# A window-attention and wavelet-convolution kernel: the keys' scaling moves from VectorE to GpSimd

## The reference, cut to what matters

```python
qkv = einsum('oc,bchw->bohw', w_qkv, gn(x))     # then cut into 16x16 windows and 8 heads of 12 channels
q = l2norm(q)                                   # over the 12 channels of a head
k = l2norm(k)                                   # k / |k|
ksum = k.sum(axis=-1) + 1e-6                    # over the 256 pixels of a window
tailor = 1.0 / (256 + einsum('bhnc,bhc->bhn', q, ksum))
kv = einsum('bhmn,bhcn->bhmc', k, v)
attn = (einsum('bhnm,bhmc->bhcn', q, kv) + v.sum(-1)) * tailor
y = batchnorm(einsum('oc,bchw->bohw', w_proj, attn)) * gamma + beta
x = x + y                                       # then layer 1
```

## Time and profile before

| | |
|---|---|
| runs | 11306.57, 11311.51, 11315.59 us (median 11311.51) |
| the profiled execution | 11311.75 us, of which the span is 11309.9 us |
| PE busy | 10853.3 us, 96% |
| DVE busy | 9314.2 us, 82% |
| ACT busy | 6979.7 us, 62% |
| POOL busy | 3419.9 us, 30% |
| attention block, first to last copy to `tok` | 131.7 to 5506.9 us |

### The profile page before, as it was taken

The page is one execution under the profiler, slowest core; times in us unless marked ns, Lnnn a source line. Parts: engine busy times, 40 slices in busy tenths (PEclk is TensorE's granted clock), DMA queues, the critical chain, the costliest instruction groups (busy, mean ns, idle before and its releaser), DMA issues.

```text
span 11309.9 us, 208798 instructions
## 1 busy us (share of the span) xinstructions
PE 10853.3 (96%) x68772; PEld 9284.1 (82%) x68772; DVE 9314.2 (82%) x16092; ACT 6979.7 (62%) x11660; POOL 3419.9 (30%) x2756
## 2 busy tenths in 40 slices
PE   4999999999999999999599999999999999999999
PEld 4888888888888888888588888888888888888888
DVE  6989999899998989988677777777777777777777
ACT  4777777777777777788445445454454545545454
POOL 3444444344444444444222122212222122221221
PEclk9999999999999999999799999999999999999999
DMA  5333233233333333222266666666666766667665
GB/s 184 126 101 125 96 123 123 92 129 101 114 114 116 113 101 130 93 80 81 73 140 151 148 148 147 145 153 147 149 145 145 154 146 150 144 146 153 145 150 118
DMA packets 1149039, 1453.41 MB, mean 129 GB/s; under 512 B 201567, under 2 KB 1111199, under 8 KB 1111455
## 3 DMA queue, kind: packets, MB, share of 16 engines
q1 hardware_dynamic: 1147231, 1442.74, 50.1%
q10 hardware_dynamic: 1376, 6.13, 0.1%
HBM read 1040.06 MB, written 408.56 MB: 128 GB/s over the span
## 4 chain that ended last, share of the span: by engine, by line
PE 49%; DVE 1%; SPq 0%; DMA 0%; issue 0%; POOL 0%; DVEq 0%; POOLq 0%
PE ps_w L1274 10%; PE ps_w L1275 10%; PE ps_w L1276 10%; PE ps_ll L1282 4%; PE ps L1274 4%; PE ps L1275 4%; PE ps L1276 4%; PE ps_w L1317 4%; DVE ob L1399 0%; DVE x L1337 0%; DMA yb<-y_scratch 0%; SPq L1101 0%; SPq L1110 0%; DMA prm<-params 0%; SPq L1120 0%
## 5 line engine op out<-in xcount | busy, mean ns | idle before, releaser
L1274 PE MATMUL ps_w<-zb,mat 128*128 128x512 f32 x4800 | 1925.7, 401 | 1.6 <-DVE ob L1399 1.6
L1276 PE MATMUL ps_w<-zb,mat 128*128 128x512 f32 x4800 | 1907.6, 397 | 0.0
L1275 PE MATMUL ps_w<-zb,mat 128*128 128x512 f32 x4800 | 1907.2, 397 | 0.0
L1227 ACT ACTIVATE z<-x,prm 64x384 f32<-64x384 f32 (+1 forms) x3072 | 1807.2, 659 | 55.5 <-DVE x L1337 47.8
L635 POOL CAST xn_hi<-xs 96x512 fp32r<-96x512 f32 x1024 | 842.7, 823 | 3106.9 <-PE ps_qkv L660 2255.4
L1173 POOL CAST mat<-raw 128x1280 fp32r<-128x1280 f32 (+1 forms) x288 | 344.8, 1215 | 4454.8 <-DMA raw<-vec 2674.2
L1399 DVE SCALAR_TENSOR_TENSOR ob<-ps_w,prm,x 64x512 f32<-64x512 f32 x1920 | 1440.6, 750 | 148.7 <-PE ps_w L1317 109.5
L1337 DVE SCALAR_TENSOR_TENSOR x<-yb,prm,xb 128x1024 f32<-128x1024 f32 (+1 forms) x576 | 1120.4, 1997 | 421.6 <-DMA prm<-params 374.9
L658 PE MATMUL ps_qkv<-wqkv_hi,xn_hi 96*128 96x288 f32 x4096 | 1388.4, 339 | 38.0 <-POOL xn_lo L637 19.8
L637 POOL TENSOR_TENSOR xn_lo<-xs,xn_hi 96x512 fp32r<-96x512 f32 x1024 | 1363.7, 1332 | 81.9
L1247 ACT ACTIVATE ll<-ps_ll 128x512 f32<-128x512 f32 x192 | 115.1, 599 | 1880.5 <-PE ps_ll L1282 1880.5
(11 more groups left out here) (183 smaller groups left out, 24815.2 us busy)
## 6 DMA issues: line engine op xcount, KB each, us to landing
xst<-in_x SPq DMA_DIRECT2D x96, 2048.0 KB, 13.8
xs<-in_x SPq DMA_DIRECT2D x128, 1536.0 KB, 8.9
y_scratch<-ys SPq DMA_DIRECT2D x128, 1536.0 KB, 9.5
out<-ob SPq DMA_DIRECT2D x768, 208.0 KB
xb<-in_x SPq DMA_DIRECT2D x576, 256.0 KB
yb<-y_scratch SPq DMA_DIRECT2D x576, 256.0 KB
raw<-vec SPq DMA_DIRECT2D x192, 320.0 KB, 5.4
raw<-vec SPq DMA_DIRECT2D x384, 160.0 KB, 4.2
```

What stands on the lines that cost most here:

```text
L1227: last = nc.scalar.activation(z[q * WROWS:(q + 1) * WROWS, ts, b, :], x1[slot(k, g)][rows, pairs, b, q::2], ACT.Identity, scale=prm[k][row ...
L1274: mm(out_, w[HI], xx[HI], start=start, stop=False)
L1275: mm(out_, w[HI], xx[LO], start=False, stop=False)
L1276: return mm(out_, w[LO], xx[HI], start=False, stop=stop)
```

## The change

Three things. `unit_k` is cut in two: DVE keeps the reciprocal (`invert_k`), and the multiplication goes to POOL, under the old name. POOL's step becomes unit_k(u-1) and then halves(u+2), where it was halves(u+1); the wait that halves makes for a slot is as before. And ACT normalises the next strip's four chunks in the steps j = 0, 1, 2, 3, where it was 0, 2, 4, 6. `invert_k` has one wait more, for POOL's multiplication of the pair before, which reads `rk`.

```diff
@@ ACT, step
-                    if j % 2 == 0 and inside_(at, -PAIRS) and (at is None or at < LAST - PAIRS):
+                    if j < 4 and (at is None or at < LAST - PAIRS):
...
-                        normalise(n + 1, (k + 1) % XS, j // 2)
+                        normalise(n + 1, (k + 1) % XS, j)
@@ POOL
+                def unit_k(u, slot):
+                    pool.wait_ge(krec_ready, u + 1)
+                    pool.wait_ge(tok_copied, u + 1)
+                    k = tok[:, slot, :, PART:PART + C].rearrange("p g (h c) -> p g h c", c=HD)
+                    nc.gpsimd.tensor_tensor(k, k, rk[:].unsqueeze(3).to_broadcast([128, TG, NH, HD]), ALU.mult
+                                            ).then_inc(khat_ready, 1)
...
                 def step(b, m, k, j, at, extra, stats):
                     n = b * STRIPS_IMG + m * XS + k
-                    if at is None or at + 1 < LAST:
-                        nn, kk = (n, k) if j + 1 < PAIRS else (n + 1, (k + 1) % XS)
-                        halves(n * PAIRS + (j + 1), nn, kk, (j + 1) % PAIRS, at is not None and at + 1 < 2)
+                    if inside_(at, 1):
+                        unit_k(n * PAIRS + (j - 1), (j - 1) % 2)
+                    if at is None or at + 2 < LAST:
+                        nn, kk = (n, k) if j + 2 < PAIRS else (n + 1, (k + 1) % XS)
+                        halves(n * PAIRS + (j + 2), nn, kk, (j + 2) % PAIRS, False)
 
                 halves(0, 0, 0, 0, True)
+                halves(1, 0, 0, 1, True)
@@ DVE
-                def unit_k(u, slot):
+                def invert_k(u, slot, first):
                     dve.wait_ge(norm_ready, u + 1)
+                    if not first:
+                        dve.wait_ge(khat_ready, u)
                     v.reciprocal(rk[:], tok[:, slot, :, QR:PART]).then_inc(krec_ready, 1)
-                    dve.wait_ge(krec_ready, u + 1)
-                    dve.wait_ge(tok_copied, u + 1)
-                    k = tok[:, slot, :, PART:PART + C].rearrange("p g (h c) -> p g h c", c=HD)
-                    v.tensor_tensor(k, k, rk[:].unsqueeze(3).to_broadcast([128, TG, NH, HD]), ALU.mult
-                                    ).then_inc(khat_ready, 1)
...
-                        unit_k(u - 1, (j - 1) % 2)
+                        invert_k(u - 1, (j - 1) % 2, at == 1)
```

## The result

The changed kernel takes 11429.79 us (median of 5 runs, 11425.38 to 11447.96) against 11315.59 (5 runs, 11306.57 to 11317.82): a ratio of 1.0105, 95% interval 1.0092 to 1.0119. It is slower, by 114 us between the medians; 405 were forecast, and the time lies 0.2 us under the lower end of the range. The profiled execution has a span of 11429.0 us, 119 more than before.

A forecast was written before the change was run, and what follows sets the result against it. PE was taken to bound the kernel, with odd steps of loaded strips bound by reciprocal, multiplication, kv_sums. Terms 94 + 55 + 276 - 20 = +405 on 11311.5 gave about 11716 us, range 11430 to 11850.

The forecast's parts named there:

- The bound: Attention block: PE bounds it, and in odd steps of loaded strips the way reciprocal, multiplication, kv_sums, making a step 0.61 longer.
- The clash with even j: Even j, every strip: count_xy on DVE blocks POOL's multiplication, so PE waits; +0.54 each, 512 times, +276 us.
- The length of the multiplication: POOL's multiplication of 384 elements: 0.99 us, from a line through L637 and a 25-element operation of the same kind.
- POOL's wake: POOL's start behind the instruction that releases it: 0.19 us, read from normalise and the cast it released.
- odd j, loaded: Odd steps of loaded strips: keys ready at 3070.92 instead of 3070.64, +0.28 each, 336 times, +94 us.
- Odd j, plain: Odd steps of plain strips: slack gone, +0.24 and 0.07 for the wait, 176 times, +55 us.
- -20: Start of each strip: earlier normalise lets the first casts come at their usual time; 0.16 x 128 = 20 us given back.
- No clash: Rival for even j: multiplication and count_xy run side by side, the even term goes; 11441 us, chance 0.12.
- POOL first: Rival for even j: POOL wins the shared path, count_xy ends 1.08 later, odd keys are late; 11711 us, chance 0.15.
- Faster: Rival: POOL multiplies at the cast's rate, 0.46 us, odd keys in loaded strips 0.25 earlier; 11208 us, chance 0.11.
- Covered and free: POOL's casts behind the multiplication, invert_k's new wait and normalise in j 0 to 3: hidden, costing nothing.
- The bounds: POOL's multiplication: 0.46 us at the cast's rate to 1.38 at that of L1178.

The follow-up runs named there:

- keys_first: The kernel before with one edit: with odd j, DVE makes the keys ahead of the two bn_stats on y; 11192.0 us, ratio 0.9888.
- mult_back: The changed kernel with the multiplication of the keys alone put back on DVE; 11297.88 us, ratio 0.9984 to the kernel before.
- one_input: The changed kernel with count_xy's product of two SBUF operands replaced by a sum over one operand; 11306.29 us, ratio 0.9993.
- keys_first_early: The edits of mult_back and keys_first together, multiplication on DVE, normalise in j 0 to 3; 11098.16 us, ratio 0.981.
- keys_first_pool: The changed kernel, multiplication on POOL, with the keys ahead of the bn_stats with odd j; 11273.07 us, ratio 0.9964.

## Why the prediction was right or wrong

**The bound** was read rightly. PE waits for keys in the odd steps of loaded strips, and the way to them is reciprocal, multiplication, `kv_sums`: keys_first took what stands ahead of that way and the wait was gone. That freeing DVE behind the reciprocal gains nothing held too: 673 us of DVE's work bought nothing.

**The clash with even j** was right as a mechanism: `count_xy` first, 0.27 behind the reciprocal, POOL behind it, with 0.15 of its start hidden in the wait (forecast 0.14), and PE waiting in a step that had 1 us of slack. Its size was off: +0.54 forecast, +0.35 measured. In the step shown, `kv_sums` is 0.24 later against its copy, not 0.47: 0.15 of the difference is the multiplication, 0.84 us and not 0.99, and 0.06 `count_xy`, 1.16 and not 1.22. The wait adds 0.08 more, forecast 0.07, and the step is 5.25 against 4.93. A blocked multiplication that began its whole length only behind `count_xy`, the reading that the prediction set aside, would have ended 0.84 or more behind it; it ended 0.69 behind.

**The length of the multiplication** is the term that failed first. I took a line through two operations with two operands. L637, on which it rests, takes 2.46 ns an element, start included, and L631 2.20; what makes the two differ, the runs don't say. By itself its 0.15 is 154 (1024 times) of the 291 us that the forecast was too high. The estimate from the Trainium skill (GPSIMD Engine Reference, Performance versus the Vector engine), 0.83, which I had set aside, was within 0.015 of the measured 0.845. By the same figure L637 would take 1.11 by my estimate, and it takes 1.26, so the agreement with L631 is no rule for both.

**POOL's wake** was the second, 0.11 too long. 0.19 was read behind ACT, on the cast that waits for two semaphores. Behind DVE it was 0.08: 3094.65 to 3094.73, 3100.88 to 3100.96. Together the two make 0.26, and that is nearly the whole of the term *odd j, loaded*: forecast +0.28 from reciprocal to keys, measured 1.25 us (3100.55 to 3101.80) against 1.24 before, +0.01 (by the median over all 336, 1.25 against 1.27). The step was then even 0.16 shorter, by the give-back. *Odd j, plain*: forecast +0.31, measured nothing (4.93), for the same 0.26. By terms: 276 became 179, 94 became -54 and 55 became 0. -20 was -17 as a whole (mult_back), but only 9 of it lies in the steps into j = 0, of which the term was made.

**What I left out** is that the steps are coupled. I wrote that the chain on DVE starts at the `kv_sums` of the step before, and then priced each step as if the one before were as ever. A wait in the even step shifts PE's next step by more than it shifts DVE's chain.

**The rivals.** *No clash* gave 11441, near the measured time, and is wrong: it leaves out 512 waits that are there and has 94 + 55 us with odd j that are not. The time alone would have confirmed it; the row of 1.69 us and one_input refute it. *POOL first* did not occur: `count_xy` took 1.16 us. *Faster* would have needed under 0.7 us with odd j; it had 0.84. *Covered and free* were the casts behind the multiplication, the new wait of `invert_k`, and normalise in j 0 to 3: mult_back bears out the last. Of the first two PE shows nothing behind the start: in the block it waited hundreds of times for the keys, but for POOL's `xn_lo` and for ACT's copy to `tok` once each, at the first pairs (who waited for whom: us in total, times, the longest).

```profile
PEld ps_g L699 <- POOL tok L631: 323.6, 830, 11.9
PE ps_g L699 <- POOL tok L631: 148.5, 450, 11.5
...
PE ps_qkv L669 <- POOL xn_lo L645: 20.0, 1, 20.0
```

**The sum redone.** With 0.84 for the multiplication and 0.08 for the wake, my own working gives 512 x 0.39 + 336 x 0.02 + 176 x 0.05 - 20 = +195. `count_xy`'s 0.06 takes 31 off (512 times), the give-back 54 (336 x 0.16), and that leaves +110, where 114 were measured. The measured values went into this sum, so that it fits says that no large term is missing, and no more. The bounds, 0.46 to 1.38 for the multiplication, held its size; the lower end of the range did not come from them but from the case without a clash, at sizes that were all too large.

## What to carry to other kernels

Moving work from a busy engine to an idle one gained nothing here, since the work stayed on the way that ends last; and it lost, since there it met an operation that shuts it out. Look first at what stands ahead of the critical result in the in-order queue: moving two `bn_stats` behind it was worth more than any change of engine (keys_first), and it made a small collision elsewhere worth removing (keys_first_early against mult_back). Price each step with the one before it as it will be, and test a fitting number by taking the supposed cause away.

## What the runs showed of the hardware

- A GpSimd multiplication of 128x384 float32 with a broadcast operand took 843 to 851 ns in 1024 of 1024 cases of one_input, in 507 of which VectorE ran a sum over one SBUF operand beside it. In the changed kernel it took 1.69 us in 507 of the 512 cases with even j, where VectorE's operation with two SBUF operands was 0.16 ahead of it. There it ended 0.69 behind that operation.
- Beside `bn_stats` with one operand it took 0.85 (keys_first_pool): that does not block it.
- GpSimd started 0.08 us behind the VectorE instruction that it waited for, against 0.19 behind a ScalarE one, on a cast that waits for two semaphores. Whether the engine or the second semaphore makes the difference, these runs don't say.
- The product and sum of two operands over 1024 columns took 1.16 us behind a reciprocal (L825 in the changed kernel) and 1.21 to 1.22 behind a multiplication (L817 in the kernel before). Why, these runs don't say.
